# Transposing the tokens of seven sequences one stage earlier, into buffers that belong to the experts

## Reference

```
h = h + attention(layernorm(h))                       # 12 heads of 16, q and k RMS-normed
xn = l2norm(layernorm(h)) * sqrt(192) * gamma_in      # "tokens" in the kernel
xg = groups of 64 tokens of xn
logits1 = xg . phi                                    # phi: 128 normed slots
disp1 = softmax over the 64 tokens; comb1 = softmax over the 128 slots
slots = disp1^T . xg;  yn = l2norm(slots) * sqrt(192) * gamma2
... second level of slots, 32 experts (w1, gelu gate, w2), and back with comb2 and comb1
```

## Time and profile before

| what | us |
|---|---|
| median of 3 runs | 562.56 (562.29 to 566.72) |
| the profiled execution, device time | 566.14 |
| its span, first to last instruction | 564.4 |
| last body of attention and its tail, first filler to the stage's end | 241.66 to 271.9 |
| `first_slots` | 272.2 to 334.3 |
| PE busy over the span | 525.0 (93%) |
| mean granted TensorE clock | 0.985 |

### The profile page before, as it was taken

How to read it: one execution, slowest core, us unless ns; L and a number is a source line. 1 busy time by engine, 2 the same in 40 slices (tenths; PEclk the granted TensorE clock), 3 DMA queues, 4 the chain that set the end, 5 groups by cost and what they waited for, 6 DMA issues and landing times. The chain is left out here.

```text
span 564.4 us, 13527 instructions
## 1 busy us (share of the span) xinstructions
PE 525.0 (93%) x5431; PEld 429.5 (76%) x5431; DVE 313.8 (56%) x738; ACT 257.1 (46%) x822; POOL 83.5 (15%) x128
## 2 busy tenths in 40 slices
PE   6999999999999999999777779899989999999997
PEld 5888888766566566667655545688869999999986
DVE  2348778767776786652235755566634344444443
ACT  1234344366656665644345737667643232232320
POOL 6480000011104304400243100001000000000000
PEclk9999999999999999999968999999989999999999
DMA  6180000000000000000600006011129989999833
GB/s 238 40 289 2 2 0 2 1 2 1 1 2 3 1 1 1 2 2 1 235 4 1 1 2 209 1 57 59 61 102 407 423 318 328 302 328 313 250 53 120
DMA packets 20721, 58.79 MB, mean 104 GB/s; under 512 B 3042, under 2 KB 9796, under 8 KB 20548
## 3 DMA queue, kind: packets, MB, share of 16 engines
q1 hardware_dynamic: 14756, 49.47, 24.4%
q0 software_dynamic: 1056, 4.33, 4.1%
q10 hardware_dynamic: 4848, 4.13, 2.5%
HBM read 53.21 MB, written 4.33 MB: 102 GB/s over the span
## 5 line engine op out<-in xcount | busy, mean ns | idle before, releaser
L2095 PE MATMUL banks<-slots_t,w 64*128 64x128 f32 x1536 | 91.4, 272 | 1.1 <-PEq L1806 1.1
L2095 PEld LDWEIGHTS banks<-slots_t,w 64*128 64x128 f32 x1536 | 90.0, 188 | 1.7 <-issue 1.4
L1138 DVE TENSOR_REDUCE qk<-banks 128x4 f32<-128x1024 f32 x48 | 58.8, 1226 | 39.5 <-PE banks L601 39.5
L2168 ACT ACTIVATE ex_gelu<-banks,b_sb 128x128 f32<-128x128 f32 x128 | 36.6, 369 | 90.2 <-PE banks L2095 90.2
L601 PE MATMUL banks<-qk_t 16*128 16x256 f32 x384 | 54.4, 400 | 2.6 <-DVE qk L1138 2.4
L608 PE MATMUL banks<-qk_t 17*128 17x256 f32 x384 | 54.4, 400 | 0.0
L2188 DVE SCALAR_TENSOR_TENSOR ex_act_t<-banks,b_sb,ex_gelu 128x128 f32<-128x128 f32 x128 | 36.1, 344 | 28.9 <-ACT ex_gelu L2168 28.9
L601 PEld LDWEIGHTS banks<-qk_t 16*128 16x128 f32 x384 | 33.2, 184 | 20.3 <-issue 13.8
L2126 PE MATMUL banks<-w,ex_act_t 64*128 64x192 f32 x512 | 47.1, 323 | 1.2 <-DVE ex_act_t L2188 1.2
L2198 DVE TENSOR_REDUCE ex_rows<-banks 128x192 f32<-128x384 f32 x32 | 17.9, 558 | 47.5 <-PE banks L2126 47.5
L2126 PEld LDWEIGHTS banks<-w,ex_act_t 64*128 64x128 f32 x512 | 41.0, 187 | 1.4 <-issue 1.4
(11 more groups left out here) (231 smaller groups left out, 1048.2 us busy)
## 6 DMA issues: line engine op xcount, KB each, us to landing
w<-in_w SPq DMA_DIRECT2D x32, 768.0 KB, 9.9
w<-in_w2e SPq DMA_DIRECT2D x32, 384.0 KB, 10.9
w_slot<-in_w_slot SPq DMA_DIRECT2D x8, 576.0 KB, 3.8
rows_scratch<-ex_rows ACTq DMA_DIRECT2D x28, 96.0 KB, 7.3
yn_all<-rows_scratch POOLq DMA_DIRECT2D x7, 384.0 KB, 9.8
out<-h SPq DMA_DIRECT2D x8, 192.0 KB, 1.9
qkv_w_sb<-in_qkv_w SPq DMA_DIRECT2D x1, 864.0 KB, 5.1
wk_t<-in_wk_t ACTq DMA_DIRECT2D x2, 289.5 KB, 3.4
```

Source lines behind the costliest of these rows:

```text
L1138: nc.vector.tensor_reduce(to, flat(MAXES[0], MAXES[1] + 1).rearrange("p (h t n) -> p h t n", h=2, n=SEQ), AX.X, ALU.max, negate=True).then ...
L2095: return nc.tensor.matmul(bank[:, j * P:(j + 1) * P], g.w1[n % BUFS][rows, first + j * P:first + (j + 1) * P], x, start=start, stop=stop, ...
L2168: nc.scalar.activation(gelu[n % 2][:, j * P:(j + 1) * P], gate_bank(n)[:, j * P:(j + 1) * P], ACT.Gelu_apprx_tanh, bias=g.t["b1"][:, n, HB ...
```

## The change

- Eight token buffers instead of four: `g.tokens` 4 to 7 are the first 386 columns of `g.w2[0..3]`.
- `make_tokens` is called with n - 3 in POOL's loop, and for 5 and 6 after it, so tokens of seven sequences (MADE_AHEAD = 7) are made in the attention stage. `make_x` is left for sequence 7 alone and stands ahead of all `scale_comb`.
- `x_t` has eight parts, in `g.w1[2]` and `g.w1[3]`. In PE's last body and tail, `tokens_last` transposes sequences 0 to 6 (three transposes each) into banks 6 and 7, where 19 fillers go away; ACT copies them out (`keep_tokens`) between its exponentials. Sequence 7 is transposed after `logits(1)` in `first_slots`, into bank 0.
- In `first_slots`, `turn`, `keep`, the three fillers and the waits on `kept` of `turn_disp` and `turn_comb` are gone.
- SP clears the old semaphores first and issues each of the four second-layer loads only when the tokens in its buffer have been read (`slots_made` 5 to 8).

```diff
+MADE_AHEAD = BATCH - 1
+def turn_tokens(nc, g, n, bank):
+    for c in range(3):
+        last = nc.tensor.transpose(g.ps[bank][:, c * P:(c + 1) * P], g.tokens[n][:, 1 + c * P:1 + (c + 1) * P],
+                                   g.ident[:, :])
+    last.then_inc(g.x_turned, 1)
+def keep_tokens(nc, act, g, n, bank):
+    act.wait_ge(g.x_turned, n + 1)
+    nc.scalar.copy(g.x_t[n][:, :, :], g.ps[bank][:, 0:3 * P].rearrange("p (c n) -> p c n", c=3)
+                   ).then_inc(g.x_kept, 1)
...
-                if n >= 4:
-                    make_tokens(n - 4)
+                if n >= 3:
+                    make_tokens(n - 3)
+            for n in range(BATCH - 3, MADE_AHEAD):
+                make_tokens(n)
...
+            def tokens_last(n, members):
+                if n == BATCH - 1:
+                    for m in members:
+                        pe.wait_ge(g.tokens_made, m + 1)
+                        if m >= 2:
+                            pe.wait_ge(g.x_kept, m - 1)
+                        turn_tokens(nc, g, m, FRONT[m % 2])
...
                 else:
                     pe.wait_ge(S["fill_kept_s"], 2 * n + 2)
-                warm(n, 0, 5)
+                    pe.wait_ge(S["fill_kept_v"], n + 1)
+                tokens_last(n, (0, 1))
                 scores_and_maxima((n - 1, 2, 1) if prev else None, nxt(0))
-                warm(n, 0, 3)
                 turn_max(n, 0)
-                warm(n, 2, 0)
+                warm(n, 2)
...
-                warm(n, 3, 2)
+                warm(n, 3)
+                tokens_last(n, (2,))
                 scores_and_maxima((n, 0, 1), nxt(1))
...
-                warm(n, 2, 2)
+                warm(n, 2)
+                tokens_last(n, (3,))
                 turn_max(n, 1)
...
                     project(n - 1)
-                warm(n, 3, 0)
+                warm(n, 3)
+                tokens_last(n, (4,))
                 scores_and_maxima((n, 1, 1), nxt(2))
...
-                warm(n, 0, 4)
+                tokens_last(n, (5,))
                 turn_max(n, 2)
...
             turn_mixed(BATCH - 1)
-            keep_busy(nc, g, 0, 3)
+            tokens_last(BATCH - 1, (6,))
             project(BATCH - 1)
...
             expo(BATCH - 1, 2, 0)
             root_out(BATCH - 2)
+            keep_tokens(nc, act, g, 5, FRONT[1])
             expo(BATCH - 1, 2, 1)
             keep_out(BATCH - 1)
             keep_mixed(BATCH - 1)
+            keep_tokens(nc, act, g, 6, FRONT[0])
             root_out(BATCH - 1)
...
-            turn(0)
-            keep_busy(nc, g, 6, 3)
-            turn(1)
             for n in range(BATCH + 3):
                 if n < BATCH:
                     logits(n)
-                if n + 2 < BATCH:
-                    turn(n + 2)
+                if n == 1:
+                    turn_last_tokens()
...
-                if n + 2 < BATCH:
-                    keep(n + 2)
+                if n == 1:
+                    keep_tokens(nc, act, g, BATCH - 1, MEANS)
...
+            g.clear_before(sp)
             for n in range(EARLY):
+                sp.wait_ge(S["slots_made"], NX + n + 1)
                 load_second_layer(sp, g, n)
-            g.clear_before(sp)
...
+            for n in range(MADE_AHEAD, BATCH):
+                make_x(n)
             for n in range(BATCH):
-                if n + NX < BATCH:
-                    make_x(n + NX)
                 scale_comb(n)
```

More of the change, by code:

```diff
@@ L317, in _ @@
                 nc.gpsimd.memset(x[:, (t + 1) * DIM - 1:(t + 1) * DIM], 1.0).then_inc(S["ones_set"], 1)
-            for s in range(NX):
+            for s in range(BATCH):
                 for col in (0, TPS * (DIM + 1) - 1):
@@ L672, in project, with warm @@
                 last.then_inc(S["projected"], 1)
[L674 to L676 removed]
+            def warm(n, first):
+                if n == 0:
                     pe.wait_ge(tok["stats_kept"], norms(LAST, 1))
                     keep_busy(nc, g, OUT[1], first)
[L679 to L680 removed]
+            def tokens_last(n, members):
[5 more added lines that the diff above has]
+                        turn_tokens(nc, g, m, FRONT[m % 2])
             def body(n):
@@ L944, in body @@
                         root_out(n - 2)
+                    if not fill:
+                        keep_tokens(nc, act, g, 0, FRONT[0])
                     expo(n - 1, 2, 1)
+                if not fill:
+                    keep_tokens(nc, act, g, 1, FRONT[1])
                 if fill:
@@ L956, in body @@
                 expo(n, 0, 1)
+                if not fill:
+                    keep_tokens(nc, act, g, 2, FRONT[0])
                 if n == 0:
@@ L964, in body @@
                 expo(n, 1, 0)
+                if not fill:
+                    keep_tokens(nc, act, g, 3, FRONT[1])
                 if fill:
@@ L969, in body @@
                     keep_fill(n + 1, 2)
+                if not fill:
+                    keep_tokens(nc, act, g, 4, FRONT[0])
                 if stat:
@@ L1315, in first_slots @@
         S = {n: sem(n) for n in (
-            "centred", "weighted", "turned", "kept", "logits",
+            "centred", "weighted", "logits",
             "maxed", "disp_exped", "comb_exped", "inverted", "combined", "disp_turned",
@@ L1338, in _, with turn_last_tokens @@
         def _(pe):
[L1339 to L1349, removed]
+            def turn_last_tokens():
+                pe.wait_ge(S["weighted"], BATCH - MADE_AHEAD)
+                turn_tokens(nc, g, BATCH - 1, MEANS)
             def logits(n):
-                pe.wait_ge(S["kept"], n + 1)
+                pe.wait_ge(g.x_kept, n + 1)
                 if n >= 2:
@@ L1450, in _ @@
             act.wait_ge(g.consts_set, 2)
-            def keep(n):
-                act.wait_ge(S["turned"], n + 1)
-                if n >= 2:
-                    act.wait_ge(S["logits"], n - 1)
-                nc.scalar.copy(x_t[n % 2][:, :, :], g.ps[TURN][:, 0:3 * P].rearrange("p (c n) -> p c n", c=3)
-                               ).then_inc(S["kept"], 1)
             def disp_exp(n):
@@ L2241, in tower @@
         g.w2 = [sb(f"w2_{b}", [P, HID // P, DIM]) for b in range(EARLY)]
+        g.tokens += [g.w2[b][:, :, :].rearrange("p a d -> p (a d)")[:, 0:TPS * (DIM + 1)] for b in range(EARLY)]
         g.w1_loaded = [sem(f"w1_loaded{b}") for b in range(BUFS)]
@@ L2250, in tower @@
                   for n in range(BATCH)]
+        g.x_t = [g.w1[2 + n // 4][:, (n % 4) * 3 * P:(n % 4 + 1) * 3 * P].rearrange("p (c n) -> p c n", c=3)
+                 for n in range(BATCH)]
+        g.tokens_made, g.x_turned, g.x_kept = sem("tokens_made"), sem("x_turned"), sem("x_kept")
         g.yn_turned, g.yn_kept_s, g.yn_kept_v = sem("yn_turned"), sem("yn_kept_s"), sem("yn_kept_v")
```

25 lines of the change are left out of this document (10 added, 15 removed).

## The result

Timed side by side, the changed kernel took 558.51 us in the median of 20 executions (555.32 to 569.94), the kernel before 564.97 (562.13 to 568.44). The ratio is 0.9884, with a 95% interval of 0.9858 to 0.9911: faster, by 6.5 us in the medians. Ratios and intervals leave out executions over 1.5% above the fastest of their kernel, here 564.35 and 569.94 us of the changed one, so a ratio can differ from the quotient of the medians. The profiled execution of the changed kernel took 559.76 us, its span 558.0.

What follows compares the result with a forecast made beforehand. PE was taken to wait in first_slots for POOL, whose scale_comb stood behind a make_x, with low clock adding time. 566.14 - 13.3 (first_slots) + 0.3 (attention) = 553.1 us, range 549.0 to 557.5.

Steps and rivals of the forecast that it cites:

- the four steps: first_slots: start 1.5 us earlier, first beat 3.73, second 5.35, five of 4.84; the stage gains 13.3 us.
- C: Rival in first_slots: something behind POOL's wait ends as late, beats stay at 5.35 us; 555.7 us, chance 0.06.
- SP's waits: Second-layer loads wait for slots_made; readers come two stages later and nobody stands behind, so cost is nothing.
- rival A: The clock still falls in first_slots, 1.6 us for one stretch, 4.7 for three; 554.7 to 557.8 us, chance 0.14.
- the part that I had called unchanged: What follows maxima(7) in first_slots, forecast to stay unchanged.
- The row of POOL's place: first_slots: 6.6 us gained from POOL's place in line and the turns, four beats going from 6.49 to 4.84.
- Attention, +0.3: Attention's cost from transposes and copies replacing fillers: +0.3 us, with bounds of -0.5 to +3.5.
- The place without a filler: Attention: sequence 4's transposes ahead of scores that had followed project at once; about 0.35 us, passed on.
- B: Rival: copies in attention's last body bind ACT, up to 3.5 us instead of 0.3; 556.3 us, chance 0.05.
- rival D: Slower: clock falls in attention's last body where transposes replace fillers; up to 17.3 us more, 570.4 us, chance 0.03.
- The median of before: Shown median 3.6 us below the profiled execution, read as fewer low-clock stretches and not subtracted; otherwise the answer is 549.5.

Runs made afterwards that it cites:

- experiment 11: The changed kernel run once more unaltered, on one chip with the version that has 13 fillers back: 562.04 us, 0.9931 to the kernel before.
- experiment 7: The changed kernel with six fillers put back at the first two places of attention's last body: 554.58 us, 0.9809 to the kernel before.
- experiment 1: The changed kernel with 13 fillers put back beside the transposes in attention's last body and tail: 552.78 us, 0.9776 to the kernel before.
- experiment 10: The changed kernel with seven fillers put back at the later places of attention's last body and tail only: 555.15 us, 0.9827 to the kernel before.
- experiment 3: The kernel before without its 19 fillers in attention's last body and tail, nothing in their place: 576.47 us, 1.0156 to the kernel before.

## Why the prediction was right in its parts and wrong in its sum

**`first_slots`, the four steps: right.** The stage's start gained 1.45 us (forecast 1.5), the first beat is 3.86 (3.73), the second 5.24 (5.35), the other five 4.84 as forecast; 33.29 us between the outer `maxima`, forecast 33.3. No copy was late, C didn't happen, and SP's waits cost nobody. The clock was full from the first beat to the last in the profiled execution, not in all: in that of experiment 11 it fell in the first beat, which took 4.81 us, so rival A happens too. It was not full "through `first_slots`": a stretch of about 3.4 us came behind `maxima(7)`, in the part that I had called unchanged, but the kernel before had one of its own further on, and that part was 1.2 us shorter after.

**The row of POOL's place: right, and more of the gain than I said.** I gave 6.6 us to POOL's place and the turns and 4.7 to the clock. The single moved line took 8.7 of 11.8. It is at least as good as the whole change (0.9841 against 0.9884 and 0.9931).

**Attention, +0.3: right for the path, if the clock holds.** 30.75 us in experiment 7 against 30.42. The place without a filler, behind `project`, cost 0.43 us of transposes (forecast 0.35), as PE's timeline of the changed kernel shows:

```profile
258.52 1.57 PE L687 MATMUL banks<-proj_t_sb,xt 96*128 96x192 f32 x8
259.93 0.49 PE L103 MATMUL banks<-ident,w 128*128 128x128 f32 x3
260.36 1.13 PE L626 MATMUL banks<-qk_t 17*128 17x256 f32 x8
```

ACT was not late for the exponentials: B is out.

**The clock in attention, rival D: the step that failed.** My term for attention was +0.3 us, with bounds of -0.5 to +3.5 and nothing for the clock; from the row maximum to the stage it took 4.5 us more. The clock stood only in D, which I put at 0.03 and left out of the range, on the argument "PE's longest new stall there is some 0.6 us [...] a third of the stall that came before a fall". The forecast of the stall was exact, 0.60 us. The inference was not: one fall behind a stall of 1.8 us says nothing of what shorter ones do. In the changed kernel the clock fell with none longer than 0.82 us, the one before `turn_max` that the fillers had covered and that I hadn't listed. I had counted the removed fillers as time on PE's path, where they were worth nothing, and not as work of PE. By the same rows I could have: five fillers (ten matmul records) took 1.38 us and three transposes 0.52 at most, which overlap further when six run in a row. D came for a part of the stretch, 10.2 us at half clock, and cost 4.2 us (34.96 - 30.75), not 17.3. D named the place, but I priced it only as a case that makes the kernel slower, and not as one that takes part of the gain. The sum also had nothing for the experts, where the profiled execution lost 2.8 us.

**The median of before.** I didn't take off the 3.6 us by which three executions stood below the profiled one. That was right: over 20 executions the median was 564.97, near the profiled 566.14. The kernel with 13 fillers takes 552.8 and 553.2 us where 553.1 was forecast, but that is another kernel, and the agreement is in part luck: the eight executions of the changed kernel with a mean clock of 0.990 or more took 555.3 to 557.1 us, 2 to 4 above the forecast. A slip in the chances changes little: B's upper end, 556.3, doesn't pass the 556.9 that I gave for "faster".

**What stays open.** The gap between the change and experiment 1 is 5.7 us in the medians. In the profiled executions, also 5.7 apart, the last body makes 4.0 of it (34.96 - 30.95) and the experts 3.3, less 1.3 us by which experiment 1 was longer in its first beat, and small differences elsewhere. Not all of the gap goes with the clock: at the same mean clock of 0.994 the changed kernel took 555.3 to 557.1 us (seven executions of 32), the one with 13 fillers 553.4 to 554.1 (three of 12). In the experts PE has these waits in the changed kernel:

```profile
PE banks L2152 <- DMA yn_all<-ex_rows: 1.9, 1, 1.9
PE banks L2113 <- PEq L1824: 1.1, 1, 1.1
PE banks L2144 <- DVE ex_act_t L2206: 1.0, 1, 1.0
PE banks L2113 <- issue: 0.6, 2, 0.3
PE banks L2144 <- issue: 0.3, 1, 0.3
```

Experiment 7 has the same list without the two last, and 1.1 us for the last DMA. Windows of the stage, the changed kernel and then experiment 1:

```profile
410.91:558.00 147.09, 140.34 (x2176) 137.72 (x2176) 58.44 (x168) 37.83 (x129) 3.49 (x7) 1.00 0.85 278
```

```profile
408.53:552.30 143.77, 138.94 (x2176) 137.12 (x2176) 58.42 (x168) 37.83 (x129) 3.51 (x7) 1.00 0.86 284
```

For the same 2176 matmul records PE was busy 1.4 us longer, in a stretch at full clock. The stage took 147.1 us in the change, 147.0 in experiment 10, 146.6 in 3, 150.7 in 11 and 143.7 to 144.4 in all others. "Issue" is time in which PE waits for nothing that the profile shows. I have no cause for it. Nor is it shown what makes the clock fall in one execution and not in the next.

## What to carry to other kernels

Fillers that are replaced have to be weighed as work, in microseconds of the engine, and not by their number or by the stalls that show: here 21 transposes were 3.1 us where 19 fillers had been 5.2, and putting 13 back took the kernel from 0.9884 to 0.9776, less than either of the two kernels. If a stretch is at full clock only because it was filled, a fall of the clock is a rival with a real chance, and its price must be in the range. Before buffers are added to free an engine, look at the order of its own list: one `scale_comb` moved ahead of a product that waits gave as much as the whole change.

## What the runs showed of the hardware that I had not expected

- The clock fell with no stall of PE longer than 0.82 us before it (PE busy for 4.58 of 6.00 us around it), and with the same rows it didn't fall in experiment 10. Once down it stayed so for 10.2 and 13.6 us, with PE busy throughout, and in experiment 3 for 34 us.
- 19 fillers, 5.2 us of products that feed nothing, were worth 10.9 us in the median (576.47 against 565.53), or 8.8 by the ratio.
- Transposes count for the clock: with twice as many it was full in the profiled execution, and the median was 552.80 us against the 558.51 and 562.04 of the change.
- A stretch at half clock can cost less than the slower matmuls alone would: by the two clock levels, work that takes 10.2 us there would take 5.1 at the full one, and the last body grew by 4.2. What hid the rest isn't shown.
- Unchanged code in the experts varied between 143.7 and 150.7 us from one version to the next, by short waits of PE for nothing that shows and by the last DMA.
